# Attention steps: order of one subtraction, one exponential, the scores and one turn, and GpSimd roundings for blocks 4 to 7

## The reference, cut to what matters

```python
def _qdq(x):
    s = jnp.maximum(jnp.max(jnp.abs(x), axis=-1, keepdims=True) / 127.0, 1e-08)
    return jnp.clip(jnp.round(x / s), -127.0, 127.0) * s

q = _qdq(x) @ _qdq(wq).T + bq          # x: layernorm of the rows
kv = cond @ wkv.T + bkv
k, v = jnp.split(kv, 2, axis=-1)
attn = jax.nn.softmax(jnp.einsum('bnhd,bmhd->bhnm', q, k) * scale, axis=-1)
o = jnp.einsum('bhnm,bmhd->bnhd', attn, v).reshape(B, N, C)
out = _qdq(o) @ _qdq(wp).T + bp
x = x + jnp.tanh(g_xattn[1]) * out
```

## Time and profile before

| what | value |
|---|---|
| median of 3 runs | 186.9 us (186.82 to 187.08) |
| profiled execution, its own time | 186.96 us |
| its span, first to last instruction | 185.0 us |
| mean granted TensorE clock | 0.997 of full speed |
| busy: PE, DVE, ACT, POOL | 92%, 82%, 60%, 55% |
| attention steps 1 to 6 (from one `a_zt_` to the next, or what follows it) | 6.46, 6.47, 7.07, 6.66, 6.49, 6.45 us |

### The profile page before, as it was taken

How to read it: one execution, slowest core, us unless ns; L and a number is a source line. 1 busy time by engine, 2 the same in 40 slices (tenths; PEclk the granted TensorE clock), 3 DMA queues, 4 the chain that set the end, 5 groups by cost and what they waited for, 6 DMA issues and landing times.

```text
span 185.0 us, 3756 instructions
## 1 busy us (share of the span) xinstructions
PE 169.5 (92%) x1208; PEld 115.7 (63%) x1208; DVE 151.6 (82%) x455; ACT 111.2 (60%) x281; POOL 102.7 (55%) x177
## 2 busy tenths in 40 slices
PE   7989999998999999989768889889899899999991
PEld 7967666668565565555456666676578557656560
DVE  0799989985589989989998899999984897785663
ACT  2465044733432445764588999997799797574440
POOL 1079999996799431510295247565333569297000
PEclk9999999999999999999999999999999999999998
DMA  5979987100000000000000000000000079949943
GB/s 164 325 231 355 378 336 261 56 0 4 0 2 0 0 2 0 0 4 0 0 0 4 2 4 0 2 4 0 4 0 4 2 149 138 169 88 177 168 142 113
DMA packets 22771, 15.19 MB, mean 82 GB/s; under 512 B 17664, under 2 KB 21344, under 8 KB 22368
## 3 DMA queue, kind: packets, MB, share of 16 engines
q1 hardware_dynamic: 22112, 13.94, 29.6%
q10 hardware_dynamic: 640, 1.02, 1.5%
HBM read 9.68 MB, written 1.07 MB: 58 GB/s over the span
## 4 chain that ended last, share of the span: by engine, by line
PE 64%; ACT 15%; DVE 8%; DMA 5%; issue 4%; SPq 1%; DVEq 0%
PE PS L1843 9%; PE PS L1875 6%; PE PS L1473 5%; PE PS L1469 5%; PE PS L1470 5%; DMA CT<-ctxr 5%; ACT R L781 4%; ACT R L786 4%; PE PS L1574 4%; PE PS L1544 4%; PE PS L1671 4%; PE PS L1687 3%; PE PS L1508 3%; PE PS L1496 3%; PE PS L1657 2%
## 5 line engine op out<-in xcount | busy, mean ns | idle before, releaser
L1156 DVE TENSOR_REDUCE SM<-PS 128x8 f32<-128x1024 f32 x16 | 18.8, 1214 | 1.3 <-PE PS L1657 1.1
L357 POOL TENSOR_TENSOR R<-CT 128x512 f32<-128x512 f32 (+1 forms) x16 | 16.1, 1005 | 6.5 <-DMA CT<-ctxr 6.5
L573 POOL TENSOR_SCALAR R<-QT,SM 128x256 bf16<-128x256 f32 x32 | 15.9, 517 | 6.0 <-DVE SM L1235 5.7
L786 ACT ACTIVATE R<-PS 128x512 f32<-128x512 f32 x32 | 18.3, 604 | 0.8 <-PE PS L1671 0.7
L1671 PE MATMUL PS<-CON,R 128*128 128x128 f32 x128 | 18.3, 275 | 0.5 <-ACT R L786 0.5
L511 POOL TENSOR_TENSOR R<-R,ROW 128x256 f32<-128x256 f32 x8 | 5.8, 734 | 21.6 <-ACT R L723 10.9
L1357 DVE TENSOR_TENSOR R<-R,PS 128x512 bf16<-128x512 f32 (+1 forms) x17 | 11.6, 684 | 7.3 <-PE PS L1843 3.7
L582 POOL TENSOR_TENSOR R<-R 128x640 f32<-128x640 f32 (+1 forms) x12 | 15.0, 1282 | 2.8 <-DVE T_R L1081 2.8
L1671 PEld LDWEIGHTS PS<-CON,R 128*128 128x128 f32 x128 | 14.3, 140 | 2.1 <-issue 1.7
L920 ACT ACTIVATE R<-PS 128x512 f32<-128x512 f32 x17 | 10.1, 595 | 9.0 <-PE PS L1843 8.8
L1843 PE MATMUL PS<-R 128*128 128x512 bf16 x60 | 15.4, 379 | 0.0
(11 more groups left out here) (172 smaller groups left out, 452.4 us busy)
## 6 DMA issues: line engine op xcount, KB each, us to landing
WST<-w SPq DMA_DIRECT2D x3, 1024.0 KB, 11.8
T_R<-lagged SPq DMA_DIRECT2D x2, 768.0 KB, 8.2
X<-x SPq DMA_DIRECT2D x2, 512.0 KB, 4.8
CT<-ctxr SPq DMA_DIRECT2D x2, 512.0 KB, 8.1
y<-X SPq DMA_DIRECT2D x8, 128.0 KB, 1.8
WQP<-wqp ACTq DMA_DIRECT2D x1, 512.0 KB, 7.3
WKV<-wkv SPq DMA_DIRECT2D x1, 512.0 KB, 10.4
R<-sw SPq DMA_DIRECT2D x3, 128.0 KB, 3.4
```

Source lines behind the costliest of these rows:

```text
L357: return eng.tensor_tensor(KV[:, h % RING, lo:hi, 0:32].rearrange("p c (i j) -> p c i j", i=4), k[:, :, 0:4].unsqueeze(3).to_broadcast([P, ...
L573: nc.gpsimd.tensor_scalar(XB[:, u % XS, j, :], MX[:, b, :], GG[:, b, e:e + 1], 1.0, ALU.mult, ALU.mult).then_inc(e_xb, 1)
L786: nc.scalar.activation(ET[:, b % 2, 4 * k:4 * k + 4, :], PS[:, 4 + k % 2, :].rearrange("p (h n) -> p h n", h=4), ACT.Exp).then_inc(a_ex, 1)
L1156: V_.tensor_reduce(MX1[:, b % 2, 8 * c:8 * c + 8], S4[:, 8 * c:8 * c + 8, :], AX.X, ALU.max, negate=True).then_inc(a_mx, 1)
```

## The change

ScalarE makes the last subtraction of a step ahead of exponential 1 in steps 1 to 6; step 7 keeps its order. TensorE computes the scores between turn 2 and turn 3 instead of behind turn 3. GpSimd rounds the input of blocks 4 to 7 (`a_round`, with a semaphore of its own, behind the output rounding of the same pass); ScalarE rounds blocks 0 to 3 as before.

```diff
+            def a_round(b):
+
+                pool.wait_ge(a_z, AZT * (b + 1) - (b + 1 - GT))
+                pool.wait_ge(a_tr, b - 1)
+                nc.gpsimd.tensor_scalar(AT_[:, b % 2, :], AZ[:, b % 2, :], AR[:, b:b + 1], ROUND_H,
+                                        ALU.mult, ALU.add).then_inc(a_zqp, 1)
...
                 if b >= 4:
                     o_round(b - 4)
+                if 3 <= b < NB - 1:
+                    a_round(b + 1)
...
                     a_q0_(s + 2)
+                if 1 <= s < NB - 1:
+                    a_last_subtract(s)
                 if s >= 1:
                     a_exp(s - 1, 1)
-                if s >= 1:
+                if s == NB - 1:
                     a_last_subtract(s)
...
-                if s + 3 < NB:
-                    a_zq_(s + 3)
+                if s == 0:
+                    a_zq_(GT - 1)
...
             def a_transpose(b):
-                pe.wait_ge(a_zq, b + 1)
+                if b < GT:
+                    pe.wait_ge(a_zq, b + 1)
+                else:
+                    pe.wait_ge(a_zqp, b - GT + 1)
...
                     a_turn(s - 1, 2)
-                    a_turn(s - 1, 3)
                 if s >= 1 and s + 1 < NB:
                     a_scores(s + 1)
+                if s >= 1:
+                    a_turn(s - 1, 3)
```

More of the change, by code:

```diff
@@ L305, in build @@
         o_qp = sem("o_qp")
+        a_zqp = sem("a_zqp")
         y_d, x3_d = sem("y_d"), sem("x3_d")
@@ L535, in rows @@
                 nc.gpsimd.tensor_scalar(NMR[:, b:b + 1], MV[:, b, 0:1], -1.0, None, ALU.mult).then_inc(a_zp, 1)
-                pool.wait_ge(a_zq, b - 1)
+                if b < GT + 2:
+                    pool.wait_ge(a_zq, b - 1)
+                else:
+                    pool.wait_ge(a_zqp, b - GT - 1)
                 pool.wait_ge(a_zp, 2 * (b - GT) + 1)
@@ L750, in a_zq_ @@
             def a_zq_(b):
-                act.wait_ge(a_z, AZT * (b + 1) - max(0, b + 1 - GT))
+                act.wait_ge(a_z, AZT * (b + 1))
                 if b >= 2:
```

## The result

The changed kernel takes 187.3 us (median of 20 runs, 186.9 to 187.49) against 186.87 us (20 runs, 186.58 to 187.41) for the kernel before. The ratio of the runs is 1.0019, 95% interval 1.0013 to 1.0025: slower by about 0.36 us, with an interval from 0.24 to 0.47 (the two medians differ by 0.43). The prediction was 187.5 us with a range from 186.5 to 187.9, a sum of +0.60 us, and a chance of 0.60 for slower by over 0.2%; the measured change lies at that bound.

The account below looks back on a forecast made before the run. A loop between ScalarE and TensorE was taken to pace the steps. Losses of 0.32 and 0.33 us in steps 4 and 5 less 0.05 in step 6 gave +0.60 us, so 187.5 us, range 186.5 to 187.9.

Parts of the forecast that it names:

- The loop and its two branches: ScalarE-TensorE loop through scores and output transposes, and ScalarE's own row, pace the steps; they meet within 0.03 us.
- the new branch that part 2 named: Subtraction, scores, turn 3, exponential 3, output reading: 4.81 us from input reading in step 4, before 4.49.
- nothing is lost or won: Steps 1 to 3: ScalarE itself needs 4.92 us, more than the new branch's 4.81, so their length stays.
- The cover of steps 1 to 3: In steps 1 to 3 exponential 3 finds its turn done 0.11 us before ScalarE is free.
- short end of the terms: Lower end of the most likely case, slower by 187.2 to 187.9 us, chance 0.53; shortest turn terms give +0.48.
- about 7.0 us: Sign of being right: length of steps 4 and 5 in the profile after, with steps 1 to 3 as before.
- Step 6: No queries made there; counted from turn 0 to output reading, 4.64 us against 4.69 before, a gain of 0.05.
- Part 3 at nothing: GpSimd's rounding of blocks 4 to 7 costs 0; tightest is block 5 with 0.80 us spare, 0.70 with hand-over.
- TensorE's own row decides: Faster rival: exponential 3 does not hold the output reading; steps 4, 5 win 0.01 each, step 6 0.38; 186.5 us, chance 0.16.
- The loss in part: Rival: a shift in step 5's start takes one of two losses; +0.3 less 0.05, about 187.15 us, chance 0.24.
- The prediction's other value: Scores to turn 3 on TensorE: 1.15 us, the scores' modelled end, in place of 1.08; sum +0.81 us.

Follow-up runs that it names:

- kernel 1: Changed kernel with steps 4 and 5 put back into the old order on ScalarE and TensorE; ratio to the kernel before 0.9988.
- kernel 5: Changed kernel with TensorE's output transposes between scores and turn 3 in steps 3 to 6, ScalarE's order left; ratio to the kernel before 1.0045.
- kernel 7: Changed kernel with exponential 1 again ahead of the last subtraction, scores still ahead of turn 3; ratio to the kernel before 1.0221.
- kernel 4: Changed kernel with, in steps 3 to 6, output transposes between scores and turn 3, output reading between exponentials 2 and 3; 185.81 us, ratio to before 0.9944.
- kernel 3: Changed kernel without GpSimd's rounding, ScalarE rounds all blocks, new order kept on ScalarE and TensorE; ratio to the kernel before 1.0021.
- kernel 8: Changed kernel with turn 3 again ahead of the scores, the subtraction still ahead of exponential 1; ratio to the kernel before 1.0070.
- kernel 2: Kernel before with only GpSimd's rounding of blocks 4 to 7 added, old order on ScalarE and TensorE; ratio to the kernel before 0.9996.

## Why the prediction was right in direction and too large

**The loop and its two branches** held. The chain of the changed kernel goes over the new branch that part 2 named, in step 4 with these terms: 115.42 - 114.17 = 1.25 (1.31 predicted), 116.70 - 115.42 = 1.28 (1.28), 117.78 - 116.70 = 1.08 (1.08), 118.47 - 117.78 = 0.69 (0.64), 118.97 - 118.47 = 0.50 (0.50). The sum is 4.80 us, predicted 4.81. Two terms missed in opposite directions (the slot by -0.06, the turn by +0.05), so that the sum comes so close is in part luck. Step 4's branch thus lost 0.31 us as far as the output reading; the step lost 0.27, as the output projection now follows the reading at once (119.40 - 118.97 = 0.43), where before TensorE was still busy with values. Kernels 1, 5 and 7 show it by undoing it and by two larger doses.

That exponential 3 holds the output reading because ScalarE's queue is in order is what kernels 4 and 5 tell apart. The Trainium skill, "PSUM — Partial Sum Buffer", section "Engine vs sequencer instructions", says that ScalarE's queue is strictly first in, first out; the trace of kernel 5 agrees: its output transposes end at 118.38 + 0.27 = 118.65, and ScalarE stands idle for 0.45 us up to 119.17, waiting for turn 3, and reads the output only behind exponential 3.

**The step that failed** is "nothing is lost or won" in steps 1 to 3. They won 0.09, 0.07 and 0.08 us, in all 0.24, and kernels 1 and 3 repeat it (0.19 and 0.21). I priced the new slot of the subtraction by the start of exponential 1 (1.31 us after the input reading). But the old exponential 1 started there because it waited for turn 1. In the trace of before turn 1 (L1671) ends at 115.27 + 0.60 = 115.87 by the profile, exponential 1 starts at 115.90, 0.43 us after the query scaling (L765):

```profile
115.27 0.60 PE L1671 MATMUL PS<-CON,R 128*128 128x128 f32 x4
115.47 0.47 ACT L765 ACTIVATE T_R<-PS,SM 128x256 f32<-128x256 f32 x1
```

The subtraction does not need that turn: in the changed kernel it starts 115.42 - 115.05 = 0.37 us after the query scaling. The rest of ScalarE's row moves up with it. In step 3, which ScalarE's own row paces, the output reading comes 112.03 - 107.18 = 4.85 us after the input reading, 4.92 before:

```profile
107.18 0.38 ACT L772 ACTIVATE R<-PS 128x256 bf16<-128x256 f16 x1
...
111.08 1.07 ACT L799 ACTIVATE R<-PS 128x512 f32<-128x512 f32 x2
112.03 0.39 ACT L824 ACTIVATE R<-PS 128x256 bf16<-128x256 f16 x1
```

The cover of steps 1 to 3, 0.11 us by the prediction, did hold; exponentials 2 and 3 are still one pair there.

From the predicted +0.60 us to +0.36 it is thus -0.24 in steps 1 to 3, -0.13 in steps 4 and 5 (+0.52 instead of +0.65), -0.02 in steps 6 and 7, and +0.15 from a gap behind the loop that nothing in the prediction foresaw. Without that gap the change would have cost 0.21 us; so the direction rests on the mechanism, but that the size came as near as it did is in part luck, as the gap made up for part of what steps 1 to 5 fell short. The prediction's "short end of the terms" is misread in its list of chances: its shortest terms give +0.48, so 187.4 and not 187.2, and the measured time lies below that. Its "about 7.0 us" for steps 4 and 5 is loose in the same way: its own sum gives 6.98 for step 4 and 6.82 for step 5, which came at 6.93 and 6.74. And exponential 1 does not end 1 us after the subtraction's start, it starts then (116.42 after 115.42) and ends at 117.04; that turn 3 could not stay in front, which was drawn from it, is borne out by kernel 8.

**Step 6** won 0.06, predicted 0.05, by two errors that cancel: its branch from turn 0 to the output reading took 132.28 - 127.61 = 4.67 us instead of 4.64, again by the turn's term, and the projection then came 0.44 us behind the reading instead of 0.47. **Step 7** won 0.01, and everything behind it moved along, apart from one gap: between the last step and the first turn behind the loop TensorE stands 0.08 us without a wait that the profile shows, and that turn pair comes 0.15 us later relative to what is in front of it than before. First the two rows of the changed kernel, then those of before:

```profile
139.50 0.41 PE L1791 MATMUL PS<-CON,QT 128*128 128x128 f32 x2
139.99 1.06 PE L1689 MATMUL PS<-CON,R 128*128 128x128 f32 x8
```

```profile
139.46 0.41 PE L1773 MATMUL PS<-CON,QT 128*128 128x128 f32 x2
139.80 1.06 PE L1671 MATMUL PS<-CON,R 128*128 128x128 f32 x8
```

The gap is in the changed kernel and in kernels 1 and 3, not in the other ones; its cause stays open. Steps 1 to 7 and the gap together are +0.21 + 0.15 = +0.36 us, inside the ratio's 0.24 to 0.47. The profiled span grew by only 0.2 us because this execution reached step 1 0.18 us earlier (94.41 against 94.59), in code that the change does not touch; over the ten traces of the study that start lies anywhere from 94.36 to 95.13.

**Part 3 at nothing** was right (kernels 2 and 3). In the changed kernel the roundings take 0.478 us each, and the tightest, of block 5, ends at 105.80 while its transposes start at 106.87:

```profile
105.32 0.48 POOL L549 TENSOR_SCALAR R<-R,SM 128x256 f32<-128x256 f32 x1 [0.27 <-DVE SM L1162]
```

No instruction waited for one.

**The rivals.** "TensorE's own row decides" named its own condition, that exponential 3 does not hold the output reading up. Kernel 4 removes that hold, and there it comes true: step 6 wins 0.44 us against before (0.38 predicted), steps 4 and 5 stay at 6.68 and 6.49 against 6.66 and 6.49 (0.01 won was predicted), and step 3 wins 0.39 beyond what the rival had looked at. "The loss in part" gave the size that came (+0.3), but not by its mechanism: both steps lost, and the other four paid back.

**The passage from scores to turn.** Turn 3 started 1.08 us after the scores' start, the term that the prediction took, and not at the scores' modelled end, 1.15. The prediction's other value came from the rule that changing the tiling mode drains TensorE (the Trainium skill, "TensorEngine Tiling (Array Packing)", section "Key Properties"); the trace shows no such pause in front of turn 3, as far as a modelled end can tell. The turn itself took 0.66 instead of 0.60 and its exponential came 0.05 us later than the prediction's term. A longer turn is not peculiar to that passage: `o_rows`, four transposes of the same shape behind the input transposes, which use the full array as it does, takes 0.66 too (at 114.14 in the changed kernel). What lengthens them no run here shows.

## What to carry to other kernels

When an instruction is moved ahead in a queue, price what is left behind it: the thing pushed back (here turn 3, then exponential 3) counts with all that stands after it in the next engine's queue, and an instruction that needs nothing of it (the output reading) can be put in front. Before pricing a slot by the row that fills it now, see whether that row itself waits for something that the new one doesn't need. Two halves of a change that lose alone, or lose together, may win with a third.

## What the runs showed of the hardware that was not expected

How long TensorE was taken by a turn (from its start to the next instruction's) went with what followed it: 0.49 us ahead of output transposes (117.78 to 118.27 in the changed kernel), 0.56 ahead of the scores (118.22 to 118.78 in kernel 8) and of the values (117.65 to 118.21 in kernel 4).

A turn released by an exponential started 0.14 us after its end (117.46 + 0.62 = 118.08 on ScalarE, 118.22 on TensorE), where the input projection follows the input reading by 0.08 (114.55 to 114.63 in the changed kernel). The trace of before has it too, in step 6: 129.02 + 0.60 = 129.62 on ScalarE, 129.77 on TensorE. The two together, 0.14 where 0.06 was taken and 0.56 where 0.49 was, are what kernel 8's sum missed. ScalarE's row of kernel 8:

```profile
117.46 0.62 ACT L799 ACTIVATE R<-PS 128x512 f32<-128x512 f32 x1
```
